# Language-model tower on one core: expert MLP units of 256 columns made units of 512 columns over paired batches

## What is computed

```python
h = _L0_tok_ref(x, emb_weight, conv_weight)      # fake-quantised embedding, causal depthwise conv, relu
h = h + _L0_attn_ref(_layernorm(h), ...)         # linear recurrence (4 heads of 64), scaled by its row maximum, C and D
h = h + _L0_ffn_ref(_layernorm(h), ...)          # the expert MLP
# inside _L0_ffn_ref, on b*s = 4096 rows of d = 128:
x_attn = normed @ attn_w.T + attn_b + xf
tok = x_attn.reshape(2, 8, 256, 128)             # 2 micro batches x 8 experts x 256 tokens
y = einsum("meth,edh->metd", gelu(einsum("meti,ehi->meth", tok, fc1_w) + fc1_b), fc2_w) + fc2_b
out = gelu(y.reshape(4096, 128) @ next_w.T + next_b)
```

## Time and profile before

| | |
|---|---|
| time, median of 3 runs | 210.72 us (210.22 to 210.72) |
| span of the profiled execution, first to last instruction | 206.2 us |
| median less that span | 4.5 us |
| PE, PEld busy | 181.0 us (88%), 163.3 us (79%) |
| DVE, ACT, POOL busy | 143.2 us (69%), 116.5 us (56%), 97.5 us (47%) |

### The profile page before, as it was taken

How to read it: one execution, slowest core, us unless ns; L and a number is a source line. 1 busy time by engine, 2 the same in 40 slices (tenths; PEclk the granted TensorE clock), 3 DMA queues, 4 the chain that set the end, 5 groups by cost and what they waited for, 6 DMA issues and landing times. The chain is left out here.

```text
span 206.2 us, 4072 instructions
## 1 busy us (share of the span) xinstructions
PE 181.0 (88%) x1407; PEld 163.3 (79%) x1407; DVE 143.2 (69%) x411; ACT 116.5 (56%) x317; POOL 97.5 (47%) x144
## 2 busy tenths in 40 slices
PE   0498999999999999999694999988979979996993
PEld 0276789999899987887594898987969969995891
DVE  1859956753444434669587685995977959569994
ACT  2037986554433355454444577847759577693771
POOL 0116644999200002239576184672843917656441
PEclk9999999999999999999999699999999999999999
DMA  5991000000000000000000000010100100010012
GB/s 137 399 423 62 3 0 5 2 0 3 0 0 3 0 0 2 3 0 0 0 3 2 0 3 0 0 51 5 51 0 3 52 0 27 27 51 2 3 52 102
DMA packets 2566, 7.60 MB, mean 37 GB/s; under 512 B 309, under 2 KB 1122, under 8 KB 2290
## 3 DMA queue, kind: packets, MB, share of 16 engines
q1 hardware_dynamic: 2258, 7.15, 9.1%
q10 hardware_dynamic: 288, 0.20, 0.4%
HBM read 5.25 MB, written 2.10 MB: 36 GB/s over the span
## 5 line engine op out<-in xcount | busy, mean ns | idle before, releaser
L421 POOL TENSOR_TENSOR hid_p<-hid_f,hid_p 128x256 fp32r<-128x256 f32 x56 | 40.2, 734 | 35.8 <-ACT hid_p L566 27.6
L564 ACT ACTIVATE hid_f<-bank,pa 128x256 f32<-128x256 f32 x64 | 30.3, 478 | 22.6 <-PE bank L1091 22.6
L1091 PE MATMUL bank<-xaT_p,fc_p 128*128 128x256 f32 x192 | 35.7, 297 | 0.8 <-ACT hid_f L564 0.7
L1111 PE MATMUL bank<-hid_p,out_hi 128*128 128x256 f32 x128 | 33.6, 288 | 0.6 <-POOL hid_p L421 0.5
L473 ACT ACTIVATE X<-bank 128x128 f32<-128x128 f32 x64 | 17.6, 279 | 23.3 <-PE bank L935 23.1
L1091 PEld LDWEIGHTS bank<-xaT_p,fc_p 128*128 128x128 f32 x192 | 27.3, 191 | 3.4 <-issue 2.0
L932 PE MATMUL bank<-uT,pa 128*128 128x128 f32 x128 | 25.1, 280 | 0.1
L843 DVE TENSOR_SCALAR xp<-h,mv,rstd 128x128 f32<-128x128 f32 x32 | 22.5, 762 | 3.3 <-POOL rstd L439 3.3
L1111 PEld LDWEIGHTS bank<-hid_p,out_hi 128*128 128x128 f32 x128 | 23.8, 188 | 1.2 <-POOL hid_p L421 0.9
L935 PE MATMUL bank<-X,pa 128*128 128x128 f32 x120 | 23.2, 275 | 0.0
L566 ACT ACTIVATE hid_p<-bank,pa 128x256 fp32r<-128x256 f32 x48 | 23.0, 478 | 0.0
(11 more groups left out here) (123 smaller groups left out, 384.4 us busy)
## 6 DMA issues: line engine op xcount, KB each, us to landing
fc_w<-in_fc SPq DMA_DIRECT2D x2, 2048.0 KB, 11.2
out<-res SPq DMA_DIRECT2D x7, 256.0 KB, 2.0
pb<-in_pack_b SPq DMA_DIRECT2D x1, 320.0 KB, 4.2
pa<-in_pack_a SPq DMA_DIRECT2D x1, 279.0 KB, 3.5
out<-res SPq DMA_DIRECT2D x2, 128.0 KB, 1.7
conv_w<-in_conv ACTq DMA_DIRECT2D x1, 128.0 KB, 3.4
pc<-in_pack_c ACTq DMA_DIRECT2D x1, 66.5 KB, 3.8
rowsel<-in_rows SPq DMA_DIRECT2D x1, 64.0 KB, 3.8
```

The costliest lines, as they stand in the source:

```text
L421: nc.gpsimd.tensor_tensor(hid_p[1][:, half, c, :], hid_f[:, m % HID_SLOTS, :], hid_p[0][:, half, c, :].bitcast(F32), ALU.subtract).then_in ...
L564: full = nc.scalar.activation(hid_f[:, m % HID_SLOTS, :], src, ACT.Gelu, bias=bias)
L1091: last = mm(bank[5 + n % 2][:, 0:HALF], fc1_p[w][:, e * HID + c * P:e * HID + (c + 1) * P], xaT_p[m][:, b % 2, half, :], start=(k == 0), s ...
L1111: last = mm(out_bank(b, half)[:, half * HALF:(half + 1) * HALF], out_p[w][:, e, c * CH:(c + 1) * CH], hid_p[m][:, half, c, :], start=(c == ...
```

## The change

The host reorders the batches to 0, 4, 1, 5, 2, 6, 3, 7, so neighbours (a **pair**) share both experts. The MLP now works in 32 **units** of 512 columns in place of 64 parts of 256: unit m belongs to expert x = m // 4 and hidden chunk m % 4, and takes the 256 tokens of both batches of pair x // 2. fc1, both gelus, the subtraction, the out product, the last gelu and the residual are all 512 wide. Even places hold an fc1 unit, odd places an out unit, `LAG` is 3 units.

A pair's units need both batches, so the MLP moves one round later: round j holds fc1 units 4(j-1) to 4(j-1)+3, round 0 has no MLP, and there is a round 8. The second passes of the scan's second group, which stood two to a place in half of round -1, are spread one to a place and reach into round 0. `hid_p` has four slots for units, `hT` six for batches; the last eight units (24 to 31) have DVE's rounding. All eight stand in rounds 7 and 8. The DMA scratch is set to 1024 bytes; the kernel issues no transfer from POOL.

```diff
+PAIRS = NB // 2
+UNITS = 2 * PAIRS * HC
 HID_SLOTS = 4
+PART_SLOTS = 4
 CORR_SLOTS = 4
-DVE_ROUND = NB - 2
-HT_SLOTS = 4
-LAG = 4
+DVE_UNIT = UNITS - 2 * HC
+HT_SLOTS = 6
+LAG = 3
+LAST_ROUND = NB
 
...
+        def unit(m):
+            x, c = divmod(m, HC)
+            pair, half = divmod(x, 2)
+            return x, pair, half, c
 
...
-            ("second", "second"), ("second", "second"), ("second", "second"), ("second", "second"),
-            ("second",), ("second",), ("second",), ("second",))
+            ("second",), ("second",), ("second",), ("second",),
+            ("second",), ("second",), ("second",), ("second",),
+            ("second",), ("second",), ("second",), ("second",),
+            (), (), (), ())
...
-        def out_bank(b, half):
-
-
-
-            if b == NB - 1:
-                return bank[half]
-            return bank[0 if b == NB - 3 else 7]
...
+        def out_bank(x):
+            return bank[{4: 0, 6: 1, 7: 0}.get(x, 7)]
...
+        def fc1_unit_of(j, n):
+            return HC * (j - 1) + n // 2 if j >= 1 and n % 2 == 0 else None
...
+                        if m is not None and (m < DVE_UNIT or m % 2 == 0):
+                            slot = m % PART_SLOTS
                             pool.wait_ge(hid_ready, m + 1)
-                            if j >= 1:
-                                pool.wait_ge(o_done, 2 * (j - 1) + half + 1)
-                            nc.gpsimd.tensor_tensor(hid_p[1][:, half, c, :], hid_f[:, m % HID_SLOTS, :],
-                                                    hid_p[0][:, half, c, :].bitcast(F32),
+                            if m >= PART_SLOTS:
+                                pool.wait_ge(out_done, m - PART_SLOTS + 1)
+                            nc.gpsimd.tensor_tensor(hid_p[1][:, slot, :], hid_f[:, m % HID_SLOTS, :],
...
+                def gelu_out(x):
+                    act.wait_ge(out_done, HC * (x + 1))
+                    if x >= 2:
+                        act.wait_ge(res_ready, x - 1)
+                    pieces = [slice(0, HALF), slice(HALF, L)] if x == NE - 1 else [slice(0, L)]
+                    for s in pieces:
+                        nc.scalar.activation(gel[:, x % 2, s], out_bank(x)[:, s], ACT.Gelu,
+                                             bias=out_c[:, x:x + 1]).then_inc(gel_ready, 1)
...
+                            src = bank[5 + m % 2][:]
 
                             full = nc.scalar.activation(hid_f[:, m % HID_SLOTS, :], src, ACT.Gelu, bias=bias)
-                            if j < DVE_ROUND:
-                                nc.scalar.activation(hid_p[0][:, half, c, :], src, ACT.Gelu,
+                            if m < DVE_UNIT:
+                                nc.scalar.activation(hid_p[0][:, m % PART_SLOTS, :], src, ACT.Gelu,
                                                      bias=bias).then_inc(hid_ready, 1)
                             else:
                                 full.then_inc(full_ready, 1)
+                            if m >= LAG and (m - LAG) % HC == HC - 1:
+                                gelu_out((m - LAG) // HC)
...
-                def high_parts(j, places):
-                    if DVE_ROUND <= j < NB:
-                        for n in places:
-                            half, c = divmod(n, HC)
-                            m = 8 * j + n
...
+                def high_part(m):
+                    slot = m % PART_SLOTS
+                    dve.wait_ge(full_ready, m + 1 - DVE_UNIT)
+                    dve.wait_ge(out_done, m - PART_SLOTS + 1)
+                    nc.vector.tensor_copy(hid_p[0][:, slot, :], hid_f[:, m % HID_SLOTS, :]).then_inc(hid_ready, 1)
...
+                def add_residual(x):
+                    pair, half = divmod(x, 2)
+                    if x >= 2:
+                        dve.wait_ge(stored[x % 2], 16 * (x // 2))
+                    dve.wait_ge(hT_ready, 2 * pair + 2)
...
+                for j in range(-3, NB - 1):
...
-                    if j >= 1:
...
+                    if j >= 2:
+                        add_residual(j - 2)
...
-                    high_parts(j, range(6, 8))
+                for m in range(DVE_UNIT, UNITS):
+                    high_part(m)
+                    if m >= LAG and (m - LAG) % HC == HC - 1:
+                        add_residual((m - LAG) // HC)
+                add_residual(NE - 1)
...
-                def fc1_part(b, n):
-                    half, c = divmod(n, HC)
-                    e = expert(b, half)
-                    if n == 0:
-                        pe.wait_ge(xaT_ready, b + 1)
-                        if b == 0:
+                def fc1_unit(m):
+                    x, pair, half, c = unit(m)
+                    if half == 0 and c == 0:
+                        pe.wait_ge(xaT_ready, 2 * pair + 2)
+                        if pair == 0:
                             pe.wait_ge(fc1_split, NE)
...
+                        if half == 0 and c == 0 and s == 1:
+                            pe.wait_ge(xaT_lo_ready, 2 * pair + 2)
+                        last = mm(bank[5 + m % 2][:], fc1_p[w][:, m * P:(m + 1) * P],
+                                  xaT_p[s][:, pair % 2, half, :, :].rearrange("p m n -> p (m n)"),
+                                  start=(k == 0), stop=(k == len(PARTS) - 1))
                     last.then_inc(fc1_done, 1)
...
-                def out_part(part):
-                    b, n = divmod(part, 8)
-                    half, c = divmod(n, HC)
-                    e = expert(b, half)
-                    if n == 0:
-
-                        if b == NB - 3:
+                def out_unit(m):
+                    x, pair, half, c = unit(m)
+                    if c == 0:
+
+                        if x == 4 or x == 6:
                             pe.wait_ge(xh_ready, NP * NB)
-                        if b >= NB - 3:
-                            pe.wait_ge(gel_ready, b - 1)
-                        elif b >= 1:
-                            pe.wait_ge(gel_ready, b)
-                    pe.wait_ge(hid_ready, part + 1)
-                    for k, (w, m) in enumerate(PARTS):
-                        if m == 1:
-                            wait_low(pe, part)
-                        last = mm(out_bank(b, half)[:, half * HALF:(half + 1) * HALF], out_p[w][:, e, c * CH:(c + 1) * CH],
-                                  hid_p[m][:, half, c, :], start=(c == 0 and k == 0),
-                                  stop=(c == HC - 1 and k == len(PARTS) - 1))
-                    if c == HC - 1:
-                        last.then_inc(o_done, 1)
+                        elif x == 5 or x == 7:
+                            pe.wait_ge(gel_ready, x - 1 if x == 5 else 5)
+                        elif x >= 1:
+                            pe.wait_ge(gel_ready, x)
+                    pe.wait_ge(hid_ready, m + 1)
+                    for k, (w, s) in enumerate(PARTS):
+                        if s == 1:
+                            wait_low(pe, m)
+                        last = mm(out_bank(x)[:], out_p[w][:, x, c * CH:(c + 1) * CH], hid_p[s][:, m % PART_SLOTS, :],
+                                  start=(c == 0 and k == 0), stop=(c == HC - 1 and k == len(PARTS) - 1))
+                    last.then_inc(out_done, 1)
 
                 def fill(j, n):
-                    if j < 0:
+                    if j <= 0:
                         for what, i in scan_work(j, n):
                             if what == "fuse":
                                 fuse(i)
                             else:
                                 {"step": scan_step, "doubling": ks_step, "second": second_pass}[what](1, i)
                     else:
-
-                        if n == LAG - 1 and j >= 1:
-                            out_part(8 * j + n - LAG)
-                        fc1_part(j, n)
-                        if n != LAG - 1 and 8 * j + n >= LAG:
-                            out_part(8 * j + n - LAG)
-
-                for j in range(-3, NB):
+                        m = HC * (j - 1) + n // 2
+                        if n % 2 == 0:
+                            fc1_unit(m)
+                        elif m >= LAG:
+                            out_unit(m - LAG)
+
+                for j in range(-3, LAST_ROUND + 1):
                     scaled, mixed, attended = j + 3, j + 2, j + 1
                     if scaled < NB:
                         transpose_x(scaled)
@@ -1158,8 +1144,8 @@
                     fill(j, 7)
                     if 0 <= mixed < NB:
                         attn(mixed)
-                for part in range(8 * NB - LAG, 8 * NB):
-                    out_part(part)
+                for m in range(UNITS - LAG, UNITS):
+                    out_unit(m)
...
+    order = np.arange(NB).reshape(2, PAIRS).T.reshape(-1)
...
+    ids = f(x)[order].reshape(NB, NCH, T).transpose(0, 2, 1)
...
+    nc = bacc.Bacc("TRN2", target_bir_lowering=False, num_devices=1, dynamic_dma_scratch_size=1024)
...
```

(1 more changed line is left out.)

165 lines of the change are left out of this document (62 added, 103 removed).

## The result

| | before | after |
|---|---|---|
| median of the runs (us) | 210.47 (208.18 to 210.72) | 218.39 (216.6 to 219.38) |
| ratio, 95% interval | 1 | 1.043 [1.037, 1.049] |
| span of the profiled execution | 206.2 | 216.6 |

What follows compares the result with a forecast made beforehand. Rounds were bound by a four-engine loop, the stretch behind the last transposition of xa by TensorE. Terms -2.1 + 2.8 + 0.35 + 1.7 + 0.4 = +3.1 gave span 209.3, plus 4.5 makes 213.8 us; range 209.0 to 218.5.

Steps and rivals of the forecast that it cites:

- the 0.216 for a matmul of 512 columns: TensorE's 512-column matmuls start 0.216 us apart; 72 behind the last transposition of xa take 15.55 us.
- Round -1 free of low parts, round 0 free of waits, L774 free in rounds 2 to 4, round 5 at 5.0: VectorE's waits on low parts: -0.9 in round -1, -1.8 in round 0, -1.6 in rounds 2 to 4, +2.1 in round 5.
- Rounds 1 to 4 ... +0.1 x 4: xp on VectorE: two instructions wait for low parts, two run free; 3.0 us instead of 2.9, +0.4 in all.
- In rounds -1 to 1 ... +0.4: Early rounds: TensorE pauses of about 2.6 us with less work between cost +0.4 us by the lower clock.
- The third rival: Matmuls of 512 columns take 0.238 us each: +1.6, giving 215.4 us; chance 0.12.
- At the end of the stream 0.2 shows: Behind the last transposition of xa, some 2 us of waits on gelus and low parts shrink to 0.2.
- +1.7: Behind the last transposition of xa: one 3.4 us stretch at the lower clock, half of it lost, +1.7 us.
- The last gelu "+0.35": At the end, behind the last matmul: two gelus in a row for all of expert 7, +0.35 us.
- The 4.5 that the median has beyond the span: Whole kernel: 4.5 us added to the forecast span of 209.3 to give the median.
- The first rival: One xp instruction waits, not two: -1.2 in each of rounds 1 to 4, one less in round 5; 208.9 us; chance 0.15.
- the rival in which POOL's fourth unit catches r_s: Rounds 1 to 4: r_s waits 1.2 us for a low part, turning -1.6 into +3.2; 218.6 us; chance 0.12.

Runs made afterwards that it cites:

- after_busy: The changed kernel with filler matmuls in TensorE's pauses: six ahead of r's transposition in rounds -1 to 2, sixteen ahead of the last transposition of xa; 213.61 us.
- after_split: The changed kernel with GpSimd's subtraction of 512 columns (the low part) written as two of 256; 213.15 us, ratio 1.020 to the kernel before.
- after_mm256: The changed kernel with each matmul of 512 columns written as two of 256, gelus and low parts unchanged; 217.78 us, ratio 1.038 to the kernel before.
- after_busy_late: The changed kernel with sixteen filler matmuls ahead of the last transposition of xa only; 215.82 us, ratio 1.024 to the kernel before.
- before_xprs: The kernel before, with GpSimd waiting for xp behind its power and for r_s before each round's first low part; 200.1 us, again 200.88.

## Why the forecast had the sign and missed the size

Three steps failed: the number of low parts that wait behind the power of round 1, the clock, and the 0.216 for a matmul of 512 columns. Point by point, measured from the first r_s on (8.17 against the forecast's 3.1, so 5.1 missed):

- **Round -1 free of low parts, round 0 free of waits, L774 free in rounds 2 to 4, round 5 at 5.0: right.** r_s took 0.17 to 0.18 for each of its instructions in every round of after. Rounds 3 and 4 (13.29 and 13.27 where 13.1 was forecast) were nearly right too, and so was round 2 without its stretch at the lower clock (13.27 in after_busy). Their xp takes 3.05, 0.23 more than before and not 0.1: **0.4 missed** in the three rounds.
- **"Rounds 1 to 4 ... +0.1 x 4": wrong in round 1.** The step that counted two units behind the power was worked out for a round in which TensorE also has out matmuls to do. Round 1 has none before its last place, so a third unit was ready. xp took 4.02, 1.2 more than the 2.81 of the kernel before and not 0.1: **1.1 missed**. With the low parts split (after_split) it is 2.81.
- **"In rounds -1 to 1 ... +0.4": the clock was mis-sized.** The two early stretches cost 1.1 and 1.4, and the one that the kernel before has in round 0 (0.7: 13.69, of which the shorter xp explains 1.69 of the 2.35 down to 11.34) is gone. That makes +1.8 where +0.4 was forecast, **1.4 missed**. The stretch in round 2 stands behind the point above, so a longer xp seems to have had a price beyond its own length. Where the stretches fall also differs between executions of nearly the same kernel (round -1 in after, round 0 in after_mm256, rounds 0 to 1 in after_busy_late), so at best their number could have been forecast: three in place of one.
- **"I take 0.216": wrong.** The reason given (a longer matmul hides the same weight load better) has little support: 0.233 against 2 x 0.119 is 0.005, and not 0.022. The third rival had the right size. 72 x 0.017 = **1.2 missed**. The row it was taken from was for another operand type, two passes in the same column time; twice the row of the very instruction was the nearer one.
- **"At the end of the stream 0.2 shows": partly.** Of the 2.0 us of waits that were to go, about 1.2 went: the 72 matmuls are 6.1 longer than the 90 and the end without the clock 4.9. **0.8 missed**, 0.35 of it the wait for the last low part.
- **"+1.7" for the clock behind the last pause: right in kind.** 1.3 measured, 0.4 too much.
- **The last gelu "+0.35": 0.59.** Adding the residual of the last expert is two instructions in a row as well (0.76, has one of 0.42). **0.2 missed**.
- **"The 4.5 that the median has beyond the span": wrongly read, and nearly without effect.** The changed kernel's profiled execution took 218.44 for a span of 216.6, so 1.8 lie beyond a span. The rest of the 4.5 was that the profile of before showed a short execution: 206.2 + 1.8 = 208.0, and the timed runs of this kernel lie between 207.9 and 211.5. The front of the span differs by 2.3 between the two profiles (first r_s at 74.78 and 77.08), and no step of the forecast concerns it.
- **The first rival's price was added wrongly**, without effect on the forecast: 1.2 in each of rounds 1 to 4 and 1.2 in round 5 are 6.0 and not 4.9, and from 0.8 to 2.0 behind the power are 1.2 and not 0.8.

Together 1.1 + 0.4 + 1.4 + 1.2 + 0.8 - 0.4 + 0.2 = 4.7 of the 5.1; the rest lies in terms of 0.1 each. The larger ones all point the same way, which their separate ranges did not provide for. The forecast's rival with units at 0.238 had 215.4; with the third unit of round 1 (1.1) and the clock (1.4) it would have been at 217.9. That 218.4 lies inside the range is luck: its upper end came from the rival in which POOL's fourth unit catches r_s (218.6), and that did not happen in after.

The front of the span deserves its rows. before_xprs was profiled twice, on two chips, 198.3 and 200.3 us long. The first execution, 18 to 22 us, and then the second:

```profile
18.00:22.00 4.00, 3.75 (x44) 3.24 (x45) 3.97 (x18) 3.34 (x9) 3.06 (x7) 1.00 0.01 2
```

```profile
18.00:22.00 4.00, 4.00 (x27) 3.17 (x26) 2.73 (x13) 2.32 (x5) 2.63 (x6) 1.00 0.00 2
```

TensorE ran 44 instructions in one and 27 in the other, and the first r_s stands at 75.11 and 77.15: all of the difference of 2.0 is the same program's front. The granted clock reads 1.00 in both, so what slows it there stays open.

## What to carry to other kernels

When work is moved to make instructions larger, ask first what the smaller ones were hiding behind, and who waits for one whole instruction of another engine: the same widening cost some 2% while VectorE sat out GpSimd's instructions and gave 2.2% when it did not. Before an operation that the critical path waits for, let the other engine wait: one line gave 3.7% to the kernel before, and a second one in the same spirit another 0.8 us by the traces, where the re-tiling itself cost time. And a term that holds for a steady round is to be worked out again for the first and the last one, where neighbours in the queue are missing.
